# A last graph pass that softmaxes its edges while it gathers them, in a two-layer graph network kernel

## The chip, the cores and the metric

One core of a Trainium2 chip runs the whole program. The metric is device time in microseconds (us) of one execution: 3219.77, the median of 3 runs (3218.48 to 3219.83). TensorE is PE, VectorE DVE, ScalarE ACT, GpSimd POOL, SyncE SP; a q behind the name is the engine's sequencer or queue.

## What is computed

3125 nodes with 256 features, 50,000 edges sorted by destination, 8 edge types. Both layers normalize x, then add a graph part and a linear-attention part; then each adds an MLP (a mixture of experts, and one for the nodes picked by top-k). The graph part of layer 0 is an attention over edges with 8 heads and typed weights; that of layer 1 is a convolution and then an attention with one head:

```python
xw = x @ W
e = leaky_relu((xw @ a_src)[src] + (xw @ a_dst)[dst], 0.2)
m = segment_max(e, dst)
ex = exp(e - m[dst]); s = segment_sum(ex, dst)
agg = segment_sum((ex / (s[dst] + 1e-16))[:, None] * xw[src], dst)
```

with a self loop added to each node. The change is about this last attention ("the last pass"), and the attention of layer 0 ("the first pass").

## The kernel before, in words

Edges lie in NB = 196 blocks of BLK = 256, each on K2 = 2 times 128 partitions. Nodes lie in NT = 25 tiles of 128. A *pair* is a block and a tile that has edges in it; there are G = NB + NT - 1 = 220. A pass goes through the pairs in order. For each block POOL issues two indirect gathers of 128 rows of the source nodes (392 in a pass); for each pair DVE multiplies the rows by the edges' weights (`weigh`), PE multiplies by a one-hot matrix of the destinations that ACT makes (`hots`, five pairs at a time, an Abs and a Relu), and DVE adds the product to the tile's sums (`add_up`, two pairs behind). Engines run in order, each through its own list, and wait on semaphores. The passes are three stages of their own, with a barrier of all engines between stages:

- `attend` (440 to 1003 us), the first pass: the softmax is done online, inside the pass. Pairs go in 14 chunks of CH = 16. Each gathered row carries the source's scores. ACT copies them out as the rows land (`fetch`, FREE = 22 pairs ahead), and the softmax of a chunk is spread over its LEAD = 6 pairs before it (`softmax`, steps i = 0 to 6): PE turns and sums the scores, DVE runs two scans under masks of where one destination ends (`mask`, which PE spreads to 16 x 8 rows with `c.slide` and `e.pair`, into PSUM), carries between blocks, exponent on ACT, back to edges (`w_kept`); step 6 makes the factor by which the old sums fade. A ring of RING = 28 blocks holds the rows. A small product (`mix`) rides along, one tile in 8 pairs.
- `convolve_and_mix` (1815 to 2312 us), which needs no softmax.
- the last pass (2362 to 2971 us): `score2` first finds each edge's source and target scores by one-hot matmuls, from index rows read back from DRAM; `segment_softmax` does the softmax of all edges at once; `aggregate` then goes through the pairs with a ring of SLOTS2 = 20 blocks, and an MLP rides along (`MlpRide`: 103 steps spread over 208 pairs, PE products with Gelu on ACT between). SP frees a block of the ring thus:

```python
if LAG <= b < NB - slots + LAG:
    pairs = sp.value_load(e.upto[0:1, b - LAG:b - LAG + 1], min_val=1, max_val=G)
    sp.wait_ge(weighted, pairs)
    sp.sem_inc(freed, 1)
```

Ahead of the last pass `gcn_to_gat` (2312 to 2362 us) makes `xw` and the two scores of each node. `find_groups` (53 to 131 us) finds blocks, pairs and masks; `project0` (165 to 440 us) makes the rows of the first pass; `route_and_share` (1003 to 1239 us) sends tokens to experts.

## Time and profile before

| | |
|---|---|
| median of 3 runs | 3219.77 us |
| the profiled execution | 3219.89 us |
| its span, first to last instruction | 3218.0 us |
| mean granted clock of PE | 0.868 |
| first pass, first gather to last matmul | 440.0 to 1001.7 us |
| last pass, first gather to last matmul | 2362.5 to 2969.5 us |

The profile is of one execution. Its 1.9 us beside the span lie before the first and behind the last instruction. Times below count from the span's start. PE, PEld (its weight load), DVE, ACT and POOL are busy only while an instruction runs; waiting and DMA issuing of SP and ACT don't count.

### The profile page before, as it was taken

To read this page: it belongs to the slowest core of one execution; us is meant where nothing else is said; L and a number is where in the kernel's file an instruction comes from. 1 tells how busy PE (TensorE), PEld (TensorE's weight loads), DVE (VectorE), ACT (ScalarE), POOL (GpSimd) and SP (SyncE) were. 2 spreads that over 40 slices of the span, in tenths; PEclk is the share of its full clock that TensorE was granted. 3 is DMA by queue.
4 is the path that set the end of the run, shared out by engine and by line. 5 is a ranking of instruction groups with operands and counts; after the bars stand their busy time and mean duration, and the time that the engine had idled before them with its cause. 6 is when DMAs were issued, how large, how long until landed. Compare 5 with 4: busy or idle time off the path is not lost. (4 is left out here: it accounts for less than half of the span.)

```text
span 3218.0 us, 44601 instructions
## 1 busy us (share of the span) xinstructions
PE 2481.7 (77%) x12282; PEld 1848.6 (57%) x12282; DVE 1432.4 (45%) x3430; ACT 1058.0 (33%) x2707; POOL 1378.1 (43%) x1389
## 2 busy tenths in 40 slices
PE   2399945777776998999995788787566788776896
PEld 2366524544544776888884455454455666554575
DVE  4664415656656220000004311233467665555767
ACT  1012224444443112232222444444410654443220
POOL 1012247777760041000004577777640677776210
PEclk7599977878877899999998799889765999998898
DMA  5035544444430013656563433333276233333101
GB/s 187 6 123 167 177 126 112 114 113 111 115 98 29 1 65 127 193 183 194 182 195 108 123 105 106 106 106 105 72 250 220 83 100 102 103 102 97 61 1 40
DMA packets 241045, 370.76 MB, mean 115 GB/s; under 512 B 65140, under 2 KB 171073, under 8 KB 240836
## 3 DMA queue, kind: packets, MB, share of 16 engines
q0 software_dynamic: 63632, 179.42, 18.9%
q1 hardware_dynamic: 147694, 157.81, 15.5%
q10 hardware_dynamic: 29510, 31.06, 2.8%
q8 instruction: 93, 1.52, 0.2%
q14 instruction: 116, 0.95, 0.1%
HBM read 306.56 MB, written 61.61 MB: 114 GB/s over the span
## 5 line engine op out<-in xcount | busy, mean ns | idle before, releaser
L1089 POOL DMA_INDIRECT ag_rows<-rows,e_bsrc x392 | 392.5, 1001 | 245.6 <-SPq L1100 109.6
L1310 POOL DMA_INDIRECT at_rows<-values,e_brow x392 | 395.1, 1008 | 144.2 <-issue 96.3
L2539 POOL DMA_INDIRECT cm_rows<-rows,e_bsrc x392 | 371.9, 949 | 145.6 <-issue 85.7
L1386 PE MATMUL at_part<-at_msg,x 128*128 128x265 f32 x880 | 279.4, 464 | 82.4 <-DVE at_msg L1541 51.1
L2619 PE MATMUL cm_part<-cm_rows,cm_one 128*128 x880 | 263.5, 436 | 100.0 <-SPq L2546 77.8
L1115 PE MATMUL banks<-ag_msg,ag_one 128*128 128x258 f32 x880 | 242.1, 410 | 103.9 <-DVE ag_msg L1148 53.9
L2619 PEld LDWEIGHTS cm_part<-cm_rows,cm_one 128*128 128x128 f32 x880 | 170.0, 210 | 185.2 <-issue 166.0
L1386 PEld LDWEIGHTS at_part<-at_msg,x 128*128 128x128 f32 x880 | 183.5, 225 | 156.2 <-DVE at_msg L1541 75.9
L2058 POOL DMA_INDIRECT je_y<-expert_out,slots x50 | 48.5, 969 | 521.6 <-POOLq L75 506.7
L1115 PEld LDWEIGHTS banks<-ag_msg,ag_one 128*128 128x128 f32 x880 | 167.1, 200 | 164.8 <-issue 74.2
L2742 DVE TENSOR_TENSOR h<-h,cm_part 128x256 f32 x220 | 92.4, 420 | 360.8 <-PE cm_part L2619 331.8
L1984 PE MATMUL x_up<-x_xt,x_w 128*128 128x256 f32 x1024 | 228.1, 381 | 7.5 <-DMA x_b<-in_L_ffn_b2p 7.5
L1995 PE MATMUL x_down<-x_w,x_hid 128*128 128x256 f32 x1024 | 229.6, 382 | 4.5 <-ACT x_hid L2014 0.6
L2035 DVE TENSOR_TENSOR x_y<-x_down,x_b 128x256 f32<-128x256 f32 x64 | 27.2, 425 | 456.7 <-PE x_down L1995 456.7
L2014 ACT ACTIVATE x_hid<-x_up,x_b 128x256 f32<-128x256 f32 x256 | 121.4, 474 | 331.9 <-PE x_up L1984 331.9
L1984 PEld LDWEIGHTS x_up<-x_xt,x_w 128*128 128x128 f32 x1024 | 195.7, 191 | 34.7 <-issue 7.8
L1995 PEld LDWEIGHTS x_down<-x_w,x_hid 128*128 128x128 f32 x1024 | 191.9, 190 | 37.1 <-ACT x_hid L2014 12.3
L2630 ACT ACTIVATE cm_one<-iota,e_local 128x128 f32<-128x128 f32 x440 | 133.2, 387 | 182.5 <-PE cm_part L2619 172.5
L830 PE MATMUL p_ring<-cat,xnt 128*128 128x512 f32 x400 | 183.5, 601 | 0.4 <-DVE p_vals L887 0.4
L1541 DVE TENSOR_TENSOR at_msg<-at_rows,at_w 128x528 f32<-128x528 f32 x220 | 155.0, 705 | 38.5 <-PE at_part L1386 18.6
L1125 ACT ACTIVATE ag_one<-iota,e_local 128x128 f32<-128x128 f32 x440 | 133.3, 387 | 116.0 <-PE banks L1115 116.0
L1396 ACT ACTIVATE x<-iota,e_local 128x128 f32<-128x128 f32 x440 | 133.3, 388 | 104.6 <-PE at_part L1386 97.1
(619 smaller groups left out, 4200.3 us busy)
## 6 DMA issues: line engine op xcount, KB each, us to landing
x_w<-in_L_ffn_W1p SPq DMA_DIRECT2D x32, 1024.0 KB
x_w<-in_L_ffn_W2p SPq DMA_DIRECT2D x32, 1024.0 KB
values<-p_hv ACTq DMA_DIRECT2D x25, 1088.0 KB, 5.0
p_brow<-local_row SPq DMA_DIRECT2D x44, 320.0 KB, 3.6
xn_acc<-local_row SPq DMA_DIRECT2D x44, 320.0 KB
xn_acc<-low_row SPq DMA_DIRECT2D x49, 256.0 KB
expert_in<-z_z POOLq DMA_DIRECT2D x8, 1024.0 KB
x_xr<-expert_in SPq DMA_DIRECT2D x32, 256.0 KB, 2.7
```

The source lines that it names most:

```text
L830: last = pe.matmul(ring[:, b, :], xnt[:, k, t * P:(t + 1) * P], cat[:, k, b * 512:(b + 1) * 512], start=(k == 0), stop=(k == DC - 1))
L1089: pool.indirect_dma_start(rows[:, b % slots, k, :], None, table, bass.IndirectOffsetOnAxis(index[:, k, b:b + 1], 0)).then_inc(gathered[b % ...
L1115: last = pe.matmul(part[:, n % deep, 0:wide], one[:, j % 2, k, u, :], msg[:, n % 4, k, :], start=(k == 0), stop=(k == K2 - 1))
L1125: last = act.activation(one[:, j % 2, k, u, :], c.iota[:], ACT.Abs, bias=e.local[:, k, j * U + u:j * U + u + 1], scale=-1.0)
L1310: pool.indirect_dma_start(rows[:, b % RING, k, :], None, table, bass.IndirectOffsetOnAxis(e.block_row[:, k, b:b + 1], 0)).then_inc(gathere ...
L1386: last = pe.matmul(part[:, n % deep, 0:wide], one[:, n // U % 2, k, n % U, :], msg[:, n % 4, k, :], start=(k == 0), stop=(k == K2 - 1))
L1396: last = act.activation(one[:, j % 2, k, u, :], c.iota[:], ACT.Abs, bias=e.local[:, k, j * U + u:j * U + u + 1], scale=-1.0)
L1541: dve.tensor_tensor(msg[:, n % 4, :, 0:VW].rearrange("p k (h w) -> p k h w", w=HW), row.rearrange("p k (h w) -> p k h w", w=HW), w[:, pc % ...
L1984: last = pe.matmul(up_ps[:, f % 3, 0:GM], w1[:, b, k, f * P:(f + 1) * P], xt[:, b, k, :], start=(k == 0), stop=(k == DC - 1))
L1995: last = pe.matmul(down_ps[:, j, 0:D], hid[:, f, j * P:(j + 1) * P], w2[:, b, f, :], start=(f == 0), stop=(f == fb - 1))
L2539: pool.indirect_dma_start(rows[:, b % SLOTS, k, :], None, table, bass.IndirectOffsetOnAxis(e.block_src[:, k, b:b + 1], 0)).then_inc(gather ...
L2619: last = pe.matmul(part[:, n % deep, :], one[:, n // U % 3, k, u, :], rows[:, bass.ds(at[u] % SLOTS, 1), k, :].squeeze(1), start=(k == 0), ...
```

## The change

The last pass becomes `attend_last`, built like `attend`: `score2`, `segment_softmax` and `aggregate` go. Rows of `rows2` get a 257th column, the source's score. `gcn_to_gat` scatters each node's two values (target score, and self-loop score) to the place of its first edge in `spread_rows` (`start`, made by ten small DVE operations and two matmuls in `route_and_share`). `attend_last` loads these, scans them along the edges (`whole`), writes them as `block_rows`, gathers them by pair, writes `pair_rows`, and each chunk loads its part. The ring has 28 blocks; the pass keeps three accumulators, two one-hot units and additions two pairs behind. In `attend` the masks come from DRAM (`pairs`, stored in `project0`) to SBUF instead of through PE to PSUM; there are five accumulators and messages, additions come four pairs behind, and three one-hot units. `find_groups` loses the masks and rows that only the old last pass used. In the ride of the MLP one accumulator stands for two. The zeroing of `expert_in` also clears `spread_rows`.

```diff
@@ -639,25 +600,6 @@
                                             step[:, h, 1:BLK + 1][:, ::-1], 0.0, ALU.min, ALU.min))
             dve.tensor_scalar(one_run[:], e.pair[:, :, 2 * BLK], 0.0, None, ALU.is_equal).then_inc(runs_made, 1)
 
-            link(dve.tensor_scalar(edge[:], edge[:], NEG, None, ALU.mult))
...
-            link(dve.tensor_scalar(e.over_this[:], this[:], -1.0, -NEG, ALU.add, ALU.mult))
             dve.wait_ge(runs_kept, 1)
...
@@ -768,11 +710,15 @@
         def _(sp):
             sp.dma_start(wq[:], a["L0_mix_W_qkv"].rearrange("(k p) j -> p k j", p=P)[:, :, 0:P]).then_inc(loaded, 16)
             sp.dma_start(wo[:], a["L0_mix_W_out"]).then_inc(loaded, 16)
+            for q in range(H0):
+                for h in range(2):
+                    sp.dma_start(pairs[h * HALF:(h + 1) * HALF, q, :], e.pair[:, h, :]).then_inc(pair_stored, 16)
             units = local_row.rearrange("(b g) e -> b (g e)", g=U)
...
             else:
                 pe.wait_ge(self.shaped, (lo // 2 + 1) * self.fb)
-                if t >= 2:
-                    pe.wait_ge(self.added, t - 1)
-                else:
-                    pe.wait_ge(*self.gate)
+                if t:
+                    pe.wait_ge(self.added, t)
                 for f in range(self.fb):
-                    last = pe.matmul(self.down_ps[:, t % 2, 0:D], self.hid[:, f, (t - lo) * P:(t - lo + 1) * P], w2[:, f, :],
...
                 if i == 0:
...
                         for k in range(K2):
                             last = pe.matmul(turn[0:q, k * P:(k + 1) * P], of[:, k].rearrange("p n h -> p (n h)"), c.ident[:],
                                              start=(n == 0 and k == 0), stop=(n == 1 and k == K2 - 1))
                     last.then_inc(scored, 1)
-                    halves = [h for h in range(2) if lo < (h + 1) * HALF and lo + m > h * HALF]
-                    for z, cut in enumerate((slice(0, BLK + 1), slice(BLK + 1, 3 * BLK + 1))):
-                        for h in halves:
-                            at = CH + lo - h * HALF
-                            last = pe.matmul(mask[0:q, z, 0:cut.stop - cut.start],
-                                             c.slide[0:HALF, at:at + m, :].rearrange("p n h -> p (n h)"),
-                                             e.pair[:, h, cut], start=(h == halves[0]), stop=(h == halves[-1]))
-                    last.then_inc(spread_out, 1)
                 if i == 1:
...
+                        last = act.activation(ones[j % 3][:, k, u, :], c.iota[:], ACT.Abs, bias=e.local[:, k, j * U + u:j * U + u + 1], scale=-1.0)
                 last.then_inc(apart, 1)
                 act.wait_ge(apart, j + 1)
-                act.activation(one[:, j % 2], one[:, j % 2], ACT.Relu, bias=c.ones[:, 0:1], scale=-1.0).then_inc(hot, 1)
+                act.activation(ones[j % 3], ones[j % 3], ACT.Relu, bias=c.ones[:, 0:1], scale=-1.0).then_inc(hot, 1)
+
+            def take_mask(pc):
+                lo, m = CHUNKS[pc]
+                act.dma_start(mask[0:m * H0, pc % 2, :], pairs[lo:lo + m].rearrange("n h w -> (n h) w")).then_inc(mask_in[pc % 2], 16)
...
+            take_mask(0)
+            take_mask(1)
...
+            hots(1)
...
+                if n >= behind_by:
+                    if (n - behind_by) % U == 0:
+                        tiles = several(nc, mybir.EngineType.DVE, e.tile, n - behind_by, U, NT)
+                    add_up(n - behind_by, tiles[(n - behind_by) % U])
+
+
+FETCHED = 8
+LAST_RING = 28
...
+def attend_last(nc, c, e, spread_rows, token_rows, block_rows, pair_rows, pairs, table, acc, ride, loads):
...
+    deep = 3
+    wide = D + 2
...
+        @block.gpsimd
+        def _(pool):
+            for h in range(2):
+                pool.indirect_dma_start(heads[:, h, :], None, token_rows, bass.IndirectOffsetOnAxis(e.head[:, h:h + 1], 0)).then_inc(heads_in, 16)
+            for b in range(NB):
+                if b == FETCHED:
+                    pool.wait_ge(block_stored, 32)
+                    for h in range(2):
+                        pool.indirect_dma_start(pair_sc[:, h, :], None, block_rows,
+                                                bass.IndirectOffsetOnAxis(e.row[0:HALF, h:h + 1], 0)).then_inc(pair_in, 16)
+                if b >= LAST_RING:
+                    pool.wait_ge(freed, b - LAST_RING + 1)
+                for k in range(K2):
+                    pool.indirect_dma_start(rows[:, b % LAST_RING, k, :], None, table,
+                                            bass.IndirectOffsetOnAxis(e.block_src[:, k, b:b + 1], 0)).then_inc(gathered[b % LAST_RING], 16)
...
+        @block.sync
+        def _(sp):
+            for h in range(2):
+                sp.dma_start(starts[:, h].rearrange("p e z -> p (e z)"),
+                             spread_rows[h * BH * BLK:(h + 1) * BH * BLK].rearrange("(b e) z -> b (e z)", e=BLK)).then_inc(spread_in, 16)
+            for to, of in loads:
+                sp.dma_start(to, of, allow_slow_non_contiguous=True).then_inc(ride_loaded, 16)
+            sp.wait_ge(filled, 4)
+            for h in range(2):
+                sp.dma_start(block_rows[h * BH:(h + 1) * BH], whole[:, h].rearrange("p z e -> p (z e)")).then_inc(block_stored, 16)
+            sp.wait_ge(pair_in, 32)
+            for h in range(2):
...
+                if i == 0:
+                    if pc:
+                        pe.wait_ge(w_kept, pc)
+                    pe.wait_ge(copied, lo + m)
+                    for k in range(K2):
+                        last = pe.transpose(turn[0:m, k * P:(k + 1) * P], src[:, pc % 2, k, 0:m], c.ident[:])
+                    last.then_inc(scored, 1)
...
+                ride.multiply(pe, n)
...
+        @block.scalar
+        def _(act):
+            def hots(j):
+                if j >= 2:
+                    act.wait_ge(multiplied, (j - 1) * U)
...
+            def take_chunk(pc):
+                lo, m = CHUNKS[pc]
+                act.dma_start(sc[0:m, pc % 2, :], pair_rows[lo:lo + m]).then_inc(chunk_in[pc % 2], 16)
+                act.dma_start(mask[0:m, pc % 2, :], pairs[lo:lo + m, 0, :]).then_inc(chunk_in[pc % 2], 16)
...
+            def fetch(n):
...
+                act.wait_ge(ready, b + 1)
+                act.copy(src[:, pc % 2, :, j:j + 1], rows[:, bass.ds(b % LAST_RING, 1), :, D:D + 1].squeeze(1)).then_inc(copied, 1)
+
+            def softmax(pc, lo, m, i):
+                if i == 3:
+                    act.wait_ge(shifted, pc + 1)
+                    act.activation(s[0:m], s[0:m], ACT.Exp, scale=-1.0).then_inc(exped, 1)
...
+                    act.activation(fade[:], small[:, 0:1], ACT.Exp).then_inc(fade_kept, 1)
...
+            for n in range(-LEAD, G):
+                if n >= 0 and n % U == 0 and n + U < G:
+                    hots(n // U + 1)
+                if n + FREE < G:
+                    fetch(n + FREE)
+                if n in step_of:
+                    softmax(*step_of[n])
+                if n >= 0:
+                    ride.shape(act, n)
...
+                    dve.tensor_tensor(fwd[0:m, :], sc[0:m, now, 0:BLK], turn[0:m, 0:BLK], ALU.add).then_inc(summed_up, 1)
+                    dve.wait_ge(summed_up, pc + 1)
+                    dve.scalar_tensor_tensor(out=s[0:m, 0, :], in0=fwd[0:m, :], scalar=SLOPE, in1=fwd[0:m, :],
+                                             op0=ALU.mult, op1=ALU.max).then_inc(leaked, 1)
+                    dve.wait_ge(leaked, pc + 1)
+                    dve.tensor_tensor_scan(fwd[0:m, :], apart_by[:, 0:BLK], s[0:m, 0, :], 0.0, ALU.add, ALU.max).then_inc(scanned, 1)
+                    dve.wait_ge(scanned, 2 * pc + 1)
+                    dve.tensor_tensor_scan(top[0:m, ::-1], apart_by[:, 1:BLK + 1][:, ::-1], fwd[0:m, ::-1], 0.0,
+                                           ALU.add, ALU.max).then_inc(scanned, 1)
...
+                    dve.wait_ge(w_kept, pc + 1)
+                row = rows[:, bass.ds(b % LAST_RING, 1), :, 0:D].squeeze(1)
+                of = w[:, pc % 2, :, j, :]
+                dve.tensor_copy(msg[:, n % 4, :, D:wide], of)
+                dve.tensor_tensor(msg[:, n % 4, :, 0:D], row, of[:, :, 0:1].broadcast_to([P, K2, D]), ALU.mult).then_inc(weighted, 1)
...
+            dve.memset(acc, 0.0).then_inc(cleared, 1)
+            dve.wait_ge(spread_in, 32)
+            dve.wait_ge(heads_in, 32)
+            dve.tensor_copy(starts[:, :, 0, :], heads[:]).then_inc(headed, 1)
+            dve.wait_ge(headed, 1)
+            for h in range(2):
+                for z in range(2):
+                    dve.tensor_tensor_scan(whole[:, h, z, :], e.keep[:, h, :], starts[:, h, :, z], 0.0, ALU.mult, ALU.add).then_inc(filled, 1)
+            dve.wait_ge(cleared, 1)
+            dve.wait_ge(pair_stored, 32)
+            dve.wait_ge(ride_loaded, 16 * len(loads))
...
+                        pe.matmul(place_ps[:, D + NT * NX:D + NT * NX + NT], c.ones[:], degree[:], start=True, stop=True).then_inc(summed, 1)
 
         @block.scalar
...
@@ -1881,6 +1900,16 @@
                 link(dve.tensor_tensor(row[:, n], row[:, n], c.valid[:], ALU.mult))
                 link(dve.tensor_tensor(row[:, n], row[:, n], spare[:, n], ALU.add))
             dve.tensor_copy(slots[:], row[:]).then_inc(placed, 1)
+            link(dve.tensor_copy(deg[:], place_ps[:, D + NT * NX:D + NT * NX + NT]))
+            link(dve.tensor_tensor_scan(before_it[:], c.ones[:, 0:NT], deg[:], 0.0, ALU.mult, ALU.add))
+            link(dve.tensor_tensor(before_it[:], before_it[:], deg[:], ALU.subtract))
...
+            link(dve.tensor_copy(start[:], before_it[:]))
...
                 dve.tensor_copy(out[:, t, :], prod[:, t % 3, 0:D + 2]).then_inc(kept, 1)
-
-            dve.memset(target[:, NT], 0.0)
...
+                    of = slice(t - U + 1, t + 1)
+                    dve.wait_ge(kept, t + 1)
+                    dve.tensor_copy(tgt[:, of, 0], out[:, of, D + 1])
...
+                    dve.wait_ge(chain, g + 1)
+                    dve.scalar_tensor_tensor(out=tgt[:, of, 1], in0=both[:, of], scalar=SLOPE, in1=both[:, of],
+                                             op0=ALU.mult, op1=ALU.max).then_inc(leaked, 1)
+
             for t in range(NT):
...
+        @block.gpsimd
+        def _(pool):
+            for t in range(NT):
+                if t % U == 0:
+                    pool.wait_ge(leaked, t // U + 1)
+                pool.indirect_dma_start(spread_rows, bass.IndirectOffsetOnAxis(start[:, t:t + 1], 0), tgt[:, t, :], None).then_inc(spread, 16)
+            pool.wait_ge(spread, 16 * NT)
...
                 sp.wait_ge(kept, lo + U)
-                sp.dma_start(table[lo * P:(lo + U) * P].rearrange("(t p) d -> p t d", p=P), out[:, lo:lo + U, 0:D]).then_inc(stored, 16)
+                sp.dma_start(table[lo * P:(lo + U) * P].rearrange("(t p) d -> p t d", p=P), out[:, lo:lo + U, 0:D + 1]).then_inc(stored, 16)
+                sp.wait_ge(leaked, lo // U + 1)
...
-                with together(nc):
-                    *made, ride_ready = score2(nc, c, e, target, own, local_row, low_row, s2, source, banks, shared, loads)
-                    gate, down_ps = segment_softmax(nc, "sm2_", c, e, 1, 2, s2, source, scores, banks, *made)
-                    aggregate(nc, "ag2_", c, e, e.block_src, rows2, 1, scores, acc, SLOTS2, banks, gate,
-                              MlpRide(xnt, x, ACT.Gelu, weights, down_ps, gate), ride_ready)
+                attend_last(nc, c, e, spread_rows, token_rows, block_rows, pair_rows, pairs, rows2, acc, MlpRide(xnt, x, ACT.Gelu, weights), loads)
```

## Rows read from the trace of the kernel before

**Rows 1.** The page: busy time of each engine over the whole span.
```profile
PE 2481.7 (77%) x12282; PEld 1848.6 (57%) x12282; DVE 1432.4 (45%) x3430; ACT 1058.0 (33%) x2707; POOL 1378.1 (43%) x1389
```
**Rows 2.** Windows: length; busy PE, PEld, DVE, ACT, POOL; PE clock, DMA share, GB/s.
```profile
967.00:1003.00 36.00, 26.70 (x94) 17.34 (x92) 24.95 (x61) 12.49 (x32) 0.00 (x0) 0.81 0.00 1
2362.00:2505.00 143.00, 78.00 (x1660) 69.25 (x1660) 107.48 (x315) 12.44 (x29) 41.86 (x40) 0.52 0.74 241
2505.00:2972.00 467.00, 367.23 (x1492) 286.86 (x1492) 271.02 (x710) 220.81 (x544) 350.69 (x352) 0.95 0.34 100
```
**Rows 3.** Single lines: min/median/max ns, first to last start, for gathers and their matmuls.
```profile
L1310 POOL DMA_INDIRECT at_rows<-values,e_brow x392: 945/949/1489, 440.0 to 952.9; - x196
L1386 PE MATMUL at_part<-at_msg,x x880: 384/388/810, 492.9 to 1001.7; 128*128 128x265 f32 x176
L2539 POOL DMA_INDIRECT cm_rows<-rows,e_bsrc x392: 945/949/966, 1815.2 to 2305.3; - x196
L1089 POOL DMA_INDIRECT ag_rows<-rows,e_bsrc x392: 945/949/1482, 2362.5 to 2963.3; - x196
L1115 PE MATMUL banks<-ag_msg,ag_one x880: 378/381/798, 2506.5 to 2969.5; 128*128 128x258 f32 x176
```
**Rows 4.** Waits in the last pass: total us, times, longest.
```profile
POOL ag_rows L1089 <- SPq L1100: 109.6, 64, 90.4
```
**Rows 5.** Waits in the first pass, the same columns.
```profile
POOL at_rows L1310 <- SPq L1321: 22.9, 75, 0.3
DVE at_s L1476 <- ACT at_slope L1426: 89.0, 13, 14.4
```
**Rows 6.** Timeline of the first pass's end: start, length, engine, line, idle before.
```profile
967.18 0.60 PE L1334 MATMUL at_turn<-ident,at_src 128*96 128x128 f32 x4
...
996.87 5.26 PE L1386 MATMUL at_part<-at_msg,x 128*128 128x265 f32 x20 [0.53 <-issue]
```
**Rows 7.** Groups by line: the work that rides along in either pass.
```profile
L1213 PE MATMUL banks<-xnt,ff_w 128*128 128x256 f32 (+1 forms) x312 | 84.4, 396 | 0.0
L1223 PE MATMUL banks<-ff_w,mr_hid 128*128 128x256 f32 x300 | 69.6, 382 | 1.2 <-ACT mr_hid L1235 1.2
L1378 PE MATMUL at_mix<-g,xnt 128*128 128x256 f32 x100 | 32.5, 455 | 0.0
```
**Rows 8.** Window of line 1115 alone: PE and PEld busy, clock, DMA.
```profile
2560.00:2580.00 20.00, 12.02 (x50) 9.31 (x50) 1.00 0.33 98
```
**Rows 9.** Timeline of ScalarE at the first Gelu of the last pass.
```profile
2517.29 1.28 ACT L1235 ACT_TABLE_LOAD   x1
2518.59 0.47 ACT L1235 ACTIVATE mr_hid<-banks,ff_b 128x256 f32<-128x256 f32 x1
```
**Rows 10.** Timeline of `gcn_to_gat`, tile 4 and the stage's last instruction.
```profile
2335.56 0.43 DVE L2427 COPY gg_out<-gg_prod 128x258 f32<-128x258 f32 x1 [0.27 <-PE gg_prod L2455]
...
2360.30 0.20 DVE L702 CAST target<-gg_rest 128x50 bf16<-128x50 f32 x1
```
**Rows 11.** A line of 50 scatters on POOL, columns as in group 3.
```profile
L1912 POOL DMA_INDIRECT expert_in<-xn,slots x50: 959/963/1080, 1155.4 to 1217.7; - x50
```
**Rows 12.** Timeline of `find_groups` around the removed stretch.
```profile
112.24 0.42 DVE L642 TENSOR_SCALAR g_edge<-g_edge 98x512 f32<-98x512 f32 x1
...
114.19 0.33 ACT L545 COPY g_runrows<-g_turn 1x220 f32<-1x220 f32 x1
...
119.31 0.24 DVE L662 MEMSET e_same<- 1x220 f32 x1
```
**Rows 13.** Timeline of `route_and_share` behind the slot chain.
```profile
1156.95 8.86 PE L1724 MATMUL ff_down<-ff_w,ff_hid 128*128 128x256 f32 x32 [1.97 <-DVE x L1791]
```
**Rows 14.** DMA issues: engine, count, KB each, median us to landing.
```profile
p_brow<-local_row SPq DMA_DIRECT2D x44, 320.0 KB, 3.6
ff_w<-in_L_mix_w_fc SPq DMA_DIRECT2D x2, 768.0 KB, 6.2
```
**Rows 15.** The first matmuls of `project0`, columns as in group 3.
```profile
L795 PE MATMUL p_ring<-cat,xnt x100: 379/379/766, 165.0 to 188.2; 128*128 128x256 f32 x100
```

800 lines of the change are left out of this document (308 added, 492 removed).

## The prediction

> **What bounds the kernel now.** The page shows no engine that is busy all the way: PE leads with 77% of the span, POOL has 43% [rows 1]. An average over such different stages decides nothing here, so I read the two changed passes by themselves, first each pass's gathers and matmuls, then the waits, then the timeline at the ends.
>
> In the first pass POOL issues 392 gathers from 440.0 to 952.9, one each 1.312 us, the last matmul starts at 1001.7 [rows 3]. Its waits for a free block are 75 times 0.3 us [rows 5], which is the plain step from one instruction to the next: POOL is never held up, and the pass is as long as its gathers (512.9) and a tail of 48.8 behind them. The tail is what the online softmax costs: pairs follow 22 behind the gathers. At chunk starts DVE waits 89.0 us in 13 times for scores that have yet to land [rows 5], so the pairs have some time to spare.
>
> In the last pass POOL starts at 2362.5, fills the ring of 20 blocks and then stands still for 90.4 us [rows 4], while DVE does `score2` and the softmax: in 2362 to 2505 POOL is busy 41.9 of 143 us [rows 2]. From 2506.5 on gathers set the pace again, until 2963.3, and the last matmul starts 6.2 us later [rows 3]. So this pass has one gather train broken by a hole, and hardly a tail: 607.0 us from the first gather to the last matmul. A gather alone costs 1.253 us in the convolution (490.1 us / 391), where DVE does little, and 1.312 in the first pass [rows 3].
>
> **The change part by part.** The sum is made against the profiled execution, 3219.9 us (0.1 over the median).
>
> *The gather train.* The hole goes; POOL issues 2 + 392 + 2 indirect DMAs. 395 intervals by 1.312 are 518.2 us; by 1.253 they would be 495. I take the first pass's step, since DVE's work is nearly the same. At block 8 POOL waits for `block_stored`. It gets there after 18 steps, 23.6 us. Ahead of it lie a clear of the sums, two loads, a copy, four short scans and two stores, which on SP's queue stand behind 1.5 MB of weights (768 KB land in 6.2 us [rows 14]): by these some 15 to 20 us. Cost nothing, up to 10 if the cover fails; the chunk data follow 30 us before they are used. The new scans under masks in SBUF read two SBUF inputs. A pass with DVE's full work has gathers 0.06 us slower than the convolution, 23 us in 392 [rows 3]; the scans are about a sixth of such work, so I price them at 4 us in the first pass, where masks came from PSUM, and count them as part of the step of 1.312 in the last. The Trainium skill, page "SBUF — State Buffer", section "Who interferes with whom", says that such a DVE instruction contends with a GpSimd one that reads SBUF. The step of 1.253 against 1.312 in rows 3 agrees. By the rule applied to every new two-input instruction, the last pass would take up to 8 us more, an estimate.
>
> *What a chunk costs.* From the turn of the last chunk's scores at 967.18 to 1001.7 the first pass runs 18 pairs and one chunk softmax with no gather in its way [rows 6, 3]: 34.5 us. Five pairs without softmax take 5.26 [rows 6], so 16 pairs with softmax are 34.5 - 2 x 1.05 = 32.4. PE is busy 26.7 of these 36 us [rows 2]; the rest is engines waiting for each other's softmax steps. The last pass puts the MLP into it: (84.4 + 69.6) / 220 = 0.70 us of PE for each pair in place of 0.15 for the mix (32.5 / 220) [rows 7], 8.8 us in a chunk. And ACT now goes between Exp and Gelu: Exp at steps 3 and 6, a Gelu in between and after, so four table loads in a chunk, 1.28 us each [rows 9], 5.1 us. Nothing hidden, a chunk costs 46.3; all hidden in the 9 us where PE idles, 32.4. PE with the MLP but no softmax runs 12.5 pairs in 20 us at full clock (50 records, four to a pair [rows 8]), 25.6 us for 16, which leaves room for about 3 of PE's own softmax work and its waits. `down` with one accumulator waits at most for DVE's add in one pair of sixteen, some 0.8 us. I take 37.5: it is nearer to the low end because PE's MLP products stand in its queue just where it waited for DVE.
>
> *The length of the last pass.* By gathers: 518.2, then 14.3 (952.9 to 967.18) and 34.5 x 37.5 / 32.4 = 39.9 behind the last: 572.4. By pairs: the first matmul comes 52.9 after the first gather [rows 3] and here 4 steps later, 58.1; then 220 / 16 = 13.75 chunks of 37.5, 515.6: 573.7. Two limits as close as these add to each other now and then; I put 5 on top: 579. Before it was 607.0: -28.0.
>
> *The start of the last pass.* Five tiles are kept at 2335.56 + 0.43 [rows 10]; three small operations later the first scatter goes, at 2336.6. Before, 50 scatters took 62.3 / 49 = 1.27 us each [rows 11]; tiles come each 1.09 us at most, so POOL sets the pace: 25 x 1.27 = 31.8, to 2368.4. With 2.8 to land and the 2.2 us between the stage's last instruction and the first gather (2360.30 to 2362.5 [rows 10, 3]) the gathers start at 2373.4: +11. Landing of 8-byte rows is not shown; 0 to 5 more.
>
> *`find_groups`.* The removed stretch on DVE runs from 112.24 to 119.31. DVE then waits for ACT's copy, which ends at 114.52 [rows 12], so 4.8 of the 7.1 us are gained. What is removed ahead of the gather of `packed` lay under that gather: nothing.
>
> *`route_and_share`.* Two small matmul groups and ten linked DVE operations come ahead of DVE's next addition, for which PE already waits 1.97 us [rows 13]: 10 x 0.22 by the tiny operations of such a chain and 0.8 for PE: +3, bounds 0 and 3.
>
> *The first pass.* POOL issues without a break, so three one-hot units and deeper accumulators can shorten only the tail. The 18 pairs could fall from 34.5 toward 18 x 1.25; the chains of the one softmax stay. I take -5 there and +4 for the masks in SBUF: -1, bounds -12 and +5. The masks' 14 loads sit on ACT's queue two chunks ahead.
>
> *`project0`, start.* SP stores 16 x 169 KB of masks ahead of the first index rows. At 3.6 us for 320 KB [rows 14] that is at most 30 us, against 23 of other work (165.0 to 188.2 [rows 15]): 0, up to +7. The clear of `spread_rows` lies under the first stage's weights. The slide matrix goes from a stage that waits for `x`: nothing.
>
> Sum: 11 - 28.0 - 4.8 + 3 - 1 = -19.8, so 3200.1.
>
> **Rivals.**
>
> *The pairs become the bound (slower).* Place: PE's and ACT's queues in `attend_last`. Beyond 37.5 us each further us per chunk costs 13.75. Everything else brings 8.2 us more than the pass's own length, so the kernel breaks even when the pass takes 598.8: at 39.3 us a chunk; by 39.8 it is slower by 0.2%. At 42, some 10 of the 13.9 us exposed, the pass takes 635.6 and the kernel 3257; with nothing hidden 694.7, 3316. For it: 26.7 of 36 us of PE [rows 2] before 8.8 are added, and ACT stopping at `hots` until PE has finished five pairs. Against it: the spare time at chunk starts [rows 5], and that MLP and pairs ran together at 1.6 us a pair [rows 8]. Here the Trainium skill speaks against the change: "ScalarE: Activation LUTs", section "What ACT_TABLE_LOAD costs", gives about 2.66 us for each switch (load and drain) and advises batching by set. By it a chunk's four switches are an estimated 10.6 us, a chunk 51.8 with nothing hidden, and the kernel about 3391. The row disagrees: the load ends at 2518.57 and the Gelu starts at 2518.59 [rows 9], so the rule gets no chance beyond this rival's.
>
> *Nearly all hides (faster than forecast).* A chunk of 34: the pass is 518.2 + 14.3 + 34.5 x 34 / 32.4 = 568.7, the first pass gains 8: 3219.9 - 38.3 + 11 - 4.8 + 3 - 8 = 3183. For it: PE waits for DVE in the softmax, and the last pass's softmax has 16 rows where the first has 128, so its turns and carries are shorter.
>
> *POOL stands at block 8.* A stall of 10 us for `block_stored` moves the whole train: 3210. For it: the stores behind 1.5 MB. Against it: 23.6 us of cover.
>
> *The hole only moves.* If gathers of the new pass were themselves late or slower (rows of 1028 bytes), the step would show it; the first pass's rows of 1088 bytes cost 0.01 us more than the last pass's of 1024 in rows 3. I give this no chance of its own.
>
> **How the numbers follow.** A pass of 565 to 592 us, the forecast: 0.48, its own range 3186 to 3213. Nearly all hides: 0.20. Block 8: 0.05. A chunk between 39 and 39.8, no change: 0.08. Pairs bound: 0.19. 0.2% is 6.4 us, about what a measurement of this kernel can tell from none. Faster, below 3213.4: 0.70, with a part of the 0.05 given away to offsets elsewhere; within 0.2%: 0.10; slower: 0.20. The predicted time is 3200. The range takes in the fast case with its bounds elsewhere, 3172, and the slow rival up to a chunk of 40.3 us, 3232; left out are the far part of the slow rival, about 0.14, and 0.04 below.
>
> **What the profile will show.** POOL's gathers of the last pass start at 2371 (2373.4 - 4.8 + 3 - 1) and run with steps of 0.3 and no wait over 1 us, block 8 included; the last one issued some 520 us after the first; the last matmul some 55 after that. DVE's longest waits at chunk starts are for scores, not for weights. About 50 table loads. The first pass keeps its 513 us of gathers, with a tail near 44. If POOL waits for SP in the last pass for tens of us, pairs are the bound and I am too low. A chunk's length without gathers, from the last chunk's turn to the end, tells it: 39.9 us for 18 pairs is the forecast.

## The result, and the profile after

The changed kernel takes 3242.8 us (median of 4 runs, 3239.2 to 3244.5) beside 3219.8 before: a ratio of 1.0069, interval 1.0052 to 1.0087. Slower by 0.7%, where I forecast 0.6% faster and gave slower a chance of 0.20. Its profiled execution took 3239.2 us, with a span of 3237.4: 19.4 more than before. All runs below but `spaced` fell on chips where the kernel before itself takes 3700 to 3730 us, so they are compared with the profile after only in stretches that run alike on both; `half` says which those are.

The page, and single lines of the two gather passes (first the gathers, then the matmuls of each pass; columns as in [rows 3]):

```profile
PE 2450.6 (76%) x10786; PEld 1818.6 (56%) x10786; DVE 1394.2 (43%) x3442; ACT 1161.4 (36%) x3011; POOL 1421.6 (44%) x1419
```

```profile
L1012 POOL DMA_INDIRECT at_rows<-values,e_brow x392: 945/949/1479, 433.3 to 947.9; - x196
...
L1079 PE MATMUL at_part<-at_msg,x x600: 384/388/810, 486.0 to 991.5; 128*128 128x265 f32 x150
...
L2447 POOL DMA_INDIRECT cm_rows<-rows,e_bsrc x392: 943/949/1222, 1809.6 to 2300.1; - x196
...
L1357 POOL DMA_INDIRECT al_rows<-rows,e_bsrc x392: 943/949/2778, 2372.8 to 2922.9; - x196
...
L1430 PE MATMUL al_part<-al_msg,al_one x880: 378/381/801, 2426.9 to 2989.6; 128*128 128x258 f32 x176
```

Against [rows 3] these starts and ends give where the 19.4 us are:

| stretch | before | after | change | forecast |
|---|---|---|---|---|
| start to the first pass's first gather (`find_groups`, `project0`) | 440.0 | 433.3 | -6.7 | -4.8 |
| first pass, first gather to last matmul | 561.7 | 558.2 | -3.5 | -1 |
| its end to the convolution's first gather (`route_and_share`) | 813.5 | 818.1 | +4.6 | +3 |
| the convolution's gathers | 490.1 | 490.5 | +0.4 | 0 |
| its last gather to the first of the last pass's train | 57.2 | 70.1 | +12.9 | +11 |
| last pass, first of the train to last matmul | 607.0 | 619.4 | +12.4 | -28 |
| the rest | 248.5 | 247.8 | -0.7 | 0 |

The last pass's train now begins with the two gathers of scores at 2370.2; from the first gather of rows, 2372.8, which the expectations below count from, the pass takes 616.8. Only one row is far off: the last pass. Its hole of 90.4 us [rows 4] is gone, as the change says, but its gathers run over 550.1 us, not some 518, and the last matmul comes 66.7 us behind the last of them. The waits show who holds them (total us, times, longest):

```profile
POOL al_rows L1357 <- issue: 104.6, 343, 0.3
...
ACT mr_hid L935 <- PE al_up L915: 71.8, 27, 7.6
...
POOL al_rows L1357 <- SPq L1379: 39.5, 49, 4.4
PE al_part L1430 <- DVE al_msg L1570: 37.9, 21, 3.2
...
PE al_down L923 <- ACT mr_hid L935: 29.3, 9, 5.3
DVE xn_acc L1578 <- ACT al_fade L1476: 26.9, 8, 5.0
DVE al_msg L1569 <- ACT al_w L1468: 20.6, 9, 3.3
```

POOL waits 49 times for SP, up to 4.4 us, that is for a free block, and so for the pairs: the sign that the prediction had named for "pairs are the bound and I am too low". From the first matmul to the last there are 562.7 us in 220 / 16 = 13.75 chunks: 40.9 us each, where I took 37.5 and had put the break-even at 39.3. That is the rival "the pairs become the bound", and with its own sum: 58.1 + 13.75 x 40.9 = 620.5, beside 619.4 measured (the first matmul came 56.7 us into the train).

The stretch of the pairs (columns as in [rows 2]), the groups of the MLP's products as in [rows 7], and its table loads:

```profile
2427.00:2990.00 563.00, 428.25 (x1674) 326.34 (x1674) 336.54 (x1019) 325.75 (x843) 365.20 (x352) 0.85 0.31 85
```

```profile
L915 PE MATMUL al_up<-xnt,ff_w 128*128 128x256 f32 (+1 forms) x312 | 96.6, 439 | 0.0
L923 PE MATMUL al_down<-ff_w,mr_hid 128*128 128x256 f32 x300 | 83.9, 438 | 29.3 <-ACT mr_hid L935 29.3
...
L935 ACT ACT_TABLE_LOAD x27 | 34.6, 1283 | 3.7 <-issue 3.3
L1463 ACT ACT_TABLE_LOAD x14 | 18.0, 1283 | 0.2
L1476 ACT ACT_TABLE_LOAD x13 | 16.7, 1283 | 0.2
```

PE is busy 428.3 of 563 us, 76%, no more than in the old pass (79% in [rows 2]), at a granted clock of 0.85 beside 0.95. The products of the MLP are the same, yet they take 439 and 438 ns each where they took 396 and 382, so the MLP holds PE (96.6 + 83.9) / 220 = 0.82 us a pair and not the 0.70 that I took from [rows 7]. There are 54 table loads, 3.9 in a chunk.

How loads and waits meet in one chunk: the timeline of all engines around a chunk's two Exps, cut to the rows that matter (columns as in [rows 6]).

```profile
2717.23 1.28 ACT L1463 ACT_TABLE_LOAD   x1
...
2718.53 0.63 ACT L1463 ACTIVATE al_s<-al_s 16x512 f32<-16x512 f32 x1
...
2719.74 3.03 ACT L1440 ACTIVATE al_one<-iota,e_local 128x128 f32<-128x128 f32 x10 [0.58 <-PE al_part L1430]
...
2722.80 1.36 ACT L1443 ACTIVATE al_one<-al_one,ones 128x1280 f32<-128x1280 f32 x1
...
2724.15 0.21 ACT L1468 COPY al_w<-al_turn 128x64 f32<-128x64 f32 x1
...
2724.46 0.32 DVE L1569 COPY al_msg<-al_w 128x4 f32<-128x4 f32 x1 [2.83 <-ACT al_w L1468]
...
2725.38 1.59 PE L1430 MATMUL al_part<-al_msg,al_one 128*128 128x258 f32 x4 [2.02 <-DVE al_msg L1570]
...
2726.34 1.28 ACT L1476 ACT_TABLE_LOAD   x1
...
2727.63 0.17 ACT L1476 ACTIVATE al_fade<-al_small 128x1 f32<-128x1 f32 x1
```

The large Exp starts only behind its load. The copy of the new weights stands behind five pairs' one-hots; DVE waits 2.83 us for it and PE 2.02 for DVE. The small Exp, on which DVE's first addition of the chunk waits, again comes behind a load.

### The profile page after: what moved, and what is told of

Same layout as the page of the kernel before. It is cut to its first block and busy times, and to the rows that moved or that the text cites. A ratio compares the mean times of both kernels' runs of the same rounds, so it can differ in the third digit from the quotient of the medians.

```text
span 3237.4 us, 41564 instructions
## 1 busy us (share of the span) xinstructions
PE 2450.6 (76%) x10786; PEld 1818.6 (56%) x10786; DVE 1394.2 (43%) x3442; ACT 1161.4 (36%) x3011; POOL 1421.6 (44%) x1419
## 3 DMA queue, kind: packets, MB, share of 16 engines
q0 software_dynamic: 64768, 180.50, 19.4%
## 5 line engine op out<-in xcount | busy, mean ns | idle before, releaser
L1357 POOL DMA_INDIRECT al_rows<-rows,e_bsrc x392 | 404.5, 1032 | 144.1 <-issue 104.6
L1430 PE MATMUL al_part<-al_msg,al_one 128*128 128x258 f32 x880 | 256.6, 432 | 50.3 <-DVE al_msg L1570 37.9
L1430 PEld LDWEIGHTS al_part<-al_msg,al_one 128*128 128x128 f32 x880 | 182.6, 215 | 91.1 <-DVE al_msg L1570 45.6
L1079 PE MATMUL at_part<-at_msg,x 128*128 128x265 f32 x600 | 185.2, 456 | 50.4 <-DVE at_msg L1243 29.9
L1079 PEld LDWEIGHTS at_part<-at_msg,x 128*128 128x128 f32 x600 | 124.4, 222 | 92.8 <-DVE at_msg L1243 39.0
L1440 ACT ACTIVATE al_one<-iota,e_local 128x128 f32<-128x128 f32 x440 | 133.2, 388 | 103.3 <-PE al_part L1430 84.3
L706 POOL TENSOR_TENSOR p_of<-p_rid,e_rel 128x640 f32<-128x640 f32 x44 | 55.5, 1262 | 251.5 <-DVE p_pick L820 193.6
```

The costliest lines, as they stand in the source:

```text
L1079: last = pe.matmul(part[:, n % deep, 0:wide], ones[n // U % 3][:, k, n % U, :], msg[:, n % ahead, k, :], start=(k == 0), stop=(k == K2 - 1))
L1357: pool.indirect_dma_start(rows[:, b % LAST_RING, k, :], None, table, bass.IndirectOffsetOnAxis(e.block_src[:, k, b:b + 1], 0)).then_inc(ga ...
L1430: last = pe.matmul(part[:, n % deep, 0:wide], one[:, n // U % 2, k, n % U, :], msg[:, n % 4, k, :], start=(k == 0), stop=(k == K2 - 1))
L1440: last = act.activation(one[:, j % 2, k, u, :], c.iota[:], ACT.Abs, bias=e.local[:, k, j * U + u:j * U + u + 1], scale=-1.0)
```

## The experiments

**`spaced`: half of the table loads gone, the MLP packed closer.**

```diff
+        free = [n for n in range(6, G - 6) if n % CH not in (13, 14, 15, 0)]
         for i, step in enumerate(steps):
-            self.due[6 + i * (G - 12) // len(steps)].append(step)
+            self.due[free[i * len(free) // len(steps)]].append(step)
```

> Edit: the changed kernel with the MLP's steps of the last pass moved: none falls on the four pairs of a chunk from the step with the large Exp to the step with the small one, so that the two Exps need one table load and the way back to Gelu another; nothing is left out. Theory T (table loads lie on a chunk's path): two of four loads of 1.28 us go, and the copy of the weights and the small Exp have no Gelu between them; a chunk falls from 40.9 by 2.5 to 4 us, the last pass from 616.8 to 570 to 585. Rival (waits between PE and ScalarE for one-hots and copies): the pass changes by under 8 us; steps packed into 12 pairs of 16 may even cost more.

This one ran where the kernel before took 3223.8 us. It took 3241.6 us.

```profile
L1431 PE MATMUL al_part<-al_msg,al_one x880: 378/382/801, 2430.8 to 2991.0; 128*128 128x258 f32 x176
```

```profile
2431.00:2991.00 560.00, 437.78 (x1673) 332.69 (x1674) 337.01 (x1019) 291.77 (x817) 369.98 (x351) 0.84 0.32 85
...
L1431 PE MATMUL al_part<-al_msg,al_one 128*128 128x258 f32 x879 | 277.3, 457 | 57.1 <-DVE al_msg L1571 42.1 <-issue 8.9 <-ACT al_one L1444 5.8
```

560.2 us of pairs, 40.7 a chunk, and 614.7 from the first gather of rows, beside 616.8, with 28 loads in the pass for 54. Theory T had asked for 2.5 to 4 us less. The window over the pairs (columns as in [rows 2]) and the group of their products (as in [rows 7]) show both a gain and a loss. PE's idle time fell from 9.8 to 8.9 us a chunk ((560.2 - 437.8) / 13.75, beside (562.7 - 428.3) / 13.75 after). Its busy time rose from 31.1 to 31.8: the pairs' own products took 457 ns each and not 432, at a granted clock of 0.84. What fewer loads gave, the packing took back.

**`noride`, `relu`, `three`, `three_b`, `noride_b`, `three_c`, `ring25`: the full pass with one thing changed.** The MLP's steps left out; Relu for Gelu; a third one-hot unit (three times); a ring of 25 blocks.

```diff
-                ride.multiply(pe, n)
...
-                if n >= 0:
-                    ride.shape(act, n)
...
-                    ride.add(dve, n)
```

```diff
-                if j >= 2:
-                    act.wait_ge(multiplied, (j - 1) * U)
+                if j >= 3:
+                    act.wait_ge(multiplied, (j - 2) * U)
...
-                if n >= 0 and n % U == 0 and n + U < G:
-                    hots(n // U + 1)
+                if n >= 0 and n % U == 0 and n + 2 * U < G:
+                    hots(n // U + 2)
```

> Edit: the changed kernel with the MLP's steps left out of the last pass (no products, no Gelu, no additions to x; its weights are still loaded). The output lacks that MLP. The last pass of the changed kernel took 616.8 us from the first gather to the last matmul, and its pairs 562.5 from first to last matmul: 40.9 a chunk of 16. Theory A (the MLP is what makes pairs the bound): a chunk needs 32 to 34 and gathers set the pace, so the last gather comes 518 to 525 after the first with no wait of POOL over 1 us, and the pass takes 565 to 580. Rival (the softmax chain with three accumulators and two one-hot units is too slow by itself): a chunk stays at 37.5 or more, POOL still waits for SP, the pass is over 590.

> Edit: the changed kernel with Relu in place of Gelu in the last pass's MLP, so that ScalarE has no table to load between it and Exp; the output has another activation there. Theory T (table loads are on the path of a chunk): four loads of 1.28 us go, 5.1 us, so a chunk falls from 40.9 to 36 and the pass from 616.8 to 575 to 585. Rival (ScalarE has slack for them, PE and the waits between engines are the bound): a chunk falls by under 1.5 us, the pass stays above 596.

> Edit: the changed kernel with a third one-hot unit in the last pass, made two units ahead of its use, as in the new first pass; everything else as it was. Theory L (ScalarE is locked to PE: it may make the next five one-hots only when PE has finished the last five, so what stands behind them in its queue, the copies that the next chunk's turn needs, comes late, 3.7 us at 2707.5): PE's wait for the copies goes, some 2 to 4 us of a chunk, and the pass falls from 616.8 to 580 to 595. Rival (table loads or the softmax's own chain): the pass changes by under 8 us.

> Edit: the same kernel as in the run named three, on another chip, since on the first one every kernel, the one before included, took some 500 us longer, with waits of 5 to 19 us all over the gathers' passes. The changed kernel with a third one-hot unit in the last pass, made two units ahead of its use. Theory L (ScalarE is locked to PE by its two units, so the copies behind them in its queue come late): the last pass falls from 616.8 to 580 to 595, the kernel's ratio to before from 1.0069 to 0.996 to 1.000. Rival (table loads, or the softmax's own chain): the pass changes by under 8 us, the ratio stays over 1.004.

> Edit: as the run named noride, since that one ran while every kernel took some 500 us longer: the MLP's steps left out of the last pass (output without that MLP). Both theories want the gathers to set the pace, 518 to 525 us with no wait of POOL over 1 us, and a pass of 565 to 580; if it stays above 590, the softmax chain alone is too slow.

> Edit: as the runs named three and three_b, which ran while every kernel took some 500 us longer: a third one-hot unit in the last pass, made two units ahead. Theory L (ScalarE locked to PE, PE waits 29 us in 12 times for the copies before a turn and 12 for one-hots): a chunk falls from 40.9 to 38 to 39.5 and the pass from 616.8 to 580 to 600. Rival: under 8 us.

> Edit: the changed kernel with a ring of 25 blocks in the last pass instead of 28; the copies run 22 pairs ahead, so 3 blocks are to spare instead of 6. Theory C (the two paces are coupled by the ring): the pass gets longer by 10 to 40 us. Theory P (pairs alone set the pace): POOL waits for blocks more often, but pairs stay within 4 us of 562.7.

On these chips every pass of gathers is stretched, the first pass and the convolution as well, which the edits don't touch (656 to 694 and 567 to 575 us of gathers, beside 515 and 490). From first gather to last matmul the last pass took 696.6 and 701.5 us without the MLP, 745.9 with Relu, 756.3, 749.6 and 755.4 with the third unit, 741.9 with the short ring. With the same kernel 7 us apart, and with no run of the changed kernel itself there, only the MLP's 50 us stand out. `three_b` was timed: 0.9984 of before, interval 0.9953 to 1.0015. The short ring (one run) is not slower than those with the long one, which speaks against a coupling through the ring, though weakly, since it was compared with runs that have a third unit. For the rest these runs are inconclusive, and the numbers expected of them, made for the other chips, can't be held against them.

**`half`: the pairs' own pace.** Half of the last pass's gathers are left out, and SP's wait for a block is set to match, so that pairs never wait for a row.

```diff
-                for k in range(K2):
+                for k in range(K2 if b < LAST_RING else 1):
                     pool.indirect_dma_start(rows[:, b % LAST_RING, k, :], None, table,
...
-                sp.wait_ge(gathered[b % LAST_RING], 16 * K2 * (b // LAST_RING + 1))
+                sp.wait_ge(gathered[b % LAST_RING], 16 * (K2 + b // LAST_RING))
```

> Edit: the changed kernel with half of the last pass's gathers left out: both rows of a block are gathered for the first 28 blocks, then only the first half of each block (the other half keeps old rows, so the sums are others). Pairs then never wait for a row, and the pass shows their own pace. Theory P (the pairs themselves are the bound, 40.9 us a chunk with nothing from the gathers): pairs stay at 555 to 563 us from first to last matmul. Theory C (pairs and gathers each need 37 to 38 a chunk and hold each other up through a ring with 6 blocks to spare): the pairs fall to 525 or less, 38 a chunk.

Two views of it: the pass's matmuls, and the window over them.

```profile
L1430 PE MATMUL al_part<-al_msg,al_one x880: 377/382/801, 2802.6 to 3355.1; 128*128 128x258 f32 x176
```

```profile
2803.00:3355.00 552.00, 425.87 (x1673) 325.17 (x1673) 335.61 (x1019) 324.65 (x841) 165.89 (x168) 0.85 0.16 42
```

552.5 us, 40.2 a chunk; busy times and clock are those of the profile after (428.3 us of PE, 0.85). The first five of the twelve intervals between the turns of successive chunks are 46.2, 40.4, 41.6, 37.4, 41.2 here and 46.9, 40.7, 41.7, 39.2, 42.6 in the profile after; the other seven differ by at most 2.2. So with few gathers the stretch runs here as it does on the other chip, and it is in such stretches that the next runs are read. Theory P is borne out, not C: the pairs alone need 40.2, 2.5 us in all under P's range, and gathers add 0.7. The 5 us that I had put on for two close limits were no longer the question, since the limits were not close.

**`half_noride`, `half_relu`, `half_three`, `half_all`, `half_defer`: what makes the 40.2.** Each is `half` with one more edit, and one execution: no MLP; Relu for Gelu; the third unit; the third unit with PE's and DVE's order changed; Gelus held back. The order of `half_all`, where the call ahead of the softmax's step takes the first layer's products alone:

```diff
-    deep = 3
+    deep, ahead, behind_by = 3, 5, 3
...
             for n in range(-LEAD, G):
+                if n > 0:
+                    ride.multiply(pe, n, False)
                 if n in step_of:
                     softmax(*step_of[n])
...
-                if n in step_of:
+                if n < 0 and n in step_of:
                     softmax(*step_of[n])
                 if 0 <= n < G:
...
                     weigh(n, blks[n % U])
+                    if n in step_of:
+                        softmax(*step_of[n])
...
-                if n >= 2:
+                if n >= behind_by:
```

and of `half_defer`:

```diff
+HELD = (13, 14, 15, 0)
...
+            while step[3] is not None and at % CH in HELD:
+                at += 1
...
-                if n >= 0:
+                if n >= 0 and (n % CH not in HELD or n > CHUNKS[-1][0]):
                     ride.shape(act, n)
+                if n > 0 and n % CH == 0:
+                    for held in range(n - 3, n + 1):
+                        ride.shape(act, held)
```

> Edit: as the run named half (half of the last pass's gathers left out, so that pairs show their own pace, 40.2 us a chunk there), and the MLP's steps left out of the last pass too. Theory M (the MLP's 8.8 us of PE work a chunk is not hidden at all): a chunk falls to 31.5 to 33, pairs 433 to 454 us in all. My forecast's rule (about half of it hides where PE waits anyway): 35 to 36.

> Edit: as half, with Relu in place of Gelu in the MLP, so no table is loaded in the pass. Theory M: under 1 us a chunk, 39.2 to 40.2. Rival T (table loads cost 5.1 a chunk in full): 35 to 36.

> Edit: as half, with a third one-hot unit, made two units ahead. Theory L (PE waits for copies and one-hots that stand behind ScalarE's wait for PE): 1.5 to 3 us less, a chunk of 37 to 38.7. Rival: within 0.7 us of 40.2. If the third unit does nothing here, it was the DVE's and PE's own order.

> Edit: as half_three, and three changes of order: the MLP's first-layer products stand ahead of the softmax's step in PE's queue, DVE weighs a pair before it takes that pair's softmax step, and its additions come three pairs behind instead of two (five messages, a ring of 27). Theory O (PE stands idle behind DVE's softmax steps because its own work is queued behind the wait, and DVE's next message is queued behind its softmax step): a chunk falls to 33 to 36. Rival (the chain of the softmax from engine to engine sets the pace whatever stands where): over 38.

> Edit: as half (half of the last pass's gathers left out), and ScalarE holds back the at most two Gelus that fall on the four pairs of a chunk from the large Exp to the small one, until after the small one; PE's products stay evenly spread, only a second-layer product may move by up to four pairs. Nothing else is left out. Theory T (the loads ahead of the two Exps are on the path, and spaced gave its gain back by packing): a chunk falls from 40.2 to 38 to 39, pairs to 523 to 537 us. Rival (two loads instead of four bring nothing, since only a pass with none lets ScalarE keep up): 39.7 to 40.5.

The window over the pairs, without the MLP, then with Relu:

```profile
2799.00:3249.00 450.00, 313.94 (x1059) 204.31 (x1058) 312.36 (x968) 223.89 (x709) 172.36 (x168) 0.78 0.19 51
```

```profile
2786.00:3293.00 507.00, 409.09 (x1673) 312.61 (x1674) 335.24 (x1019) 255.59 (x789) 167.36 (x168) 0.88 0.17 46
```

The groups of PE in the same two windows: the pairs' own products without the MLP, then with Relu, then the MLP's two layers with Relu.

```profile
L1429 PE MATMUL al_part<-al_msg,al_one 128*128 128x258 f32 x877 | 294.0, 483 | 85.9 <-DVE al_msg L1567 63.1 <-issue 13.5 <-ACT al_one L1442 8.2
```

```profile
L1430 PE MATMUL al_part<-al_msg,al_one 128*128 128x258 f32 x879 | 251.4, 425 | 50.2 <-DVE al_msg L1570 36.2 <-issue 7.7 <-ACT al_one L1443 6.2
L915 PE MATMUL al_up<-xnt,ff_w 128*128 128x256 f32 (+1 forms) x312 | 94.5, 432 | 0.0
L923 PE MATMUL al_down<-ff_w,mr_hid 128*128 128x256 f32 x300 | 73.0, 395 | 8.8 <-ACT mr_hid L935 5.2 <-issue 3.5 <-DVE x L945 0.2
```

| run | first to last matmul | a chunk | PE busy | PE idle | loads |
|---|---|---|---|---|---|
| `half_noride` | 2798.5 to 3249.4 | 32.8 | 22.8 | 10.0 | 1 |
| `half_relu` | 2786.0 to 3293.1 | 36.9 | 29.8 | 7.1 | 1 |
| `half_defer` | 2803.0 to 3336.3 | 38.8 | 29.9 | 8.9 | 28 |
| `half` | 2802.6 to 3355.1 | 40.2 | 31.0 | 9.2 | 54 |
| `half_three` | 2790.3 to 3347.0 | 40.5 | 31.2 | 9.3 | 54 |
| `half_all` | 2803.2 to 3354.8 | 40.1 | 30.7 | 9.4 | 54 |

(Columns three to five in us, by 13.75 chunks; the loads are those of the pass, and the one load of the first two runs comes ahead of the first matmul.) The MLP with Relu costs 36.9 - 32.8 = 4.1 us a chunk, Gelu's loads 40.2 - 36.9 = 3.3. `half_noride` lies in the range of theory M, but M gave the loads under 1 us and its rival T 5.1; 3.3 is neither.

Held back, half of the loads are gone and 1.4 of the 3.3 with them, as theory T expected. The edit also moves second-layer products by up to four pairs, so not all of the 1.4 need be the loads'. `spaced` had seemed to refute T; it lost to slower products what it gained in idle time.

The third unit brings nothing, so theory L falls. Theory O was not tested cleanly. `half_all` lets additions come three pairs behind but keeps three accumulators. PE's product of a pair then needs the addition of the third pair before it, which stands in DVE's queue behind the step of the softmax, and a new wait takes the place of the one for messages, 37.0 us in `half`:

```profile
PE al_part L1434 <- DVE xn_acc L1586: 54.3, 36, 3.7
```

Whether the order would help with a fourth accumulator was not run.

**`defer`, `defer_b`: the held-back Gelus with all gathers.**

> Edit: the same on the changed kernel with all of its gathers and nothing left out. Theory T: where a chunk takes 40.9 now, it takes 38.5 to 39.7, so the last pass falls by 15 to 30 us and the kernel comes to within 0.3% of the kernel before on either side, instead of 0.7% over it. Rival: no change from 1.0069.

> Edit: the same kernel as in the run named defer. By half_defer a chunk needs 38.8 us beside 40.2, so pairs still set the pace over the gathers' 37.1 to 37.7: on a chip where the kernel before takes 3220 us, the last pass falls from 616.8 to 595 to 605 and the ratio to before from 1.0069 to 1.001 to 1.004; where it takes some 3700, a ratio of 0.995 to 1.000 as before.

0.9978 of before (0.9949 to 1.0006), then 0.9964 (0.9939 to 0.9989), where before takes 3706 and 3727 us. The second is the only interval on such chips that lies below 1; it overlaps that of `three_b`, so a gain over the changed kernel is not shown there. Whether it is faster where before takes 3220 was not measured; by 38.8 + 0.7 a chunk the pass would take 54.1 + 543.1 = 597.2, and the span 3237.4 - 19.6 = 3217.8, as much as before (an estimate).

**`first`, `first_b`: the change's first pass alone on the kernel before.**

> Edit: the kernel before with the change's first pass alone: masks stored to DRAM and loaded in chunks to SBUF, five accumulators and messages, additions four pairs behind, three one-hot units; the last pass and its preparation are those of before. In the changed kernel the first pass's tail fell from 48.8 to 43.6 and its gathers took 1.7 us more, so 3.5 us are expected here, a ratio of 0.9989; storing the masks costs nothing or up to 3 us. If the first pass brought something of the 23 us of loss, this would be slower than before; I expect it is not.

> Edit: the same kernel as in the run named first, the change's first pass alone on the kernel before. On a chip where the kernel before takes 3220 us: 3.5 us less, a ratio of 0.9985 to 0.9995; elsewhere no difference from before beyond its interval.

1.0019 (0.9997 to 1.0042) and 1.0029 (1.0000 to 1.0058). The gain expected of `first` did not show there; if anything these runs are 0.2% slower. The 3.5 us of the profile after are one execution's, on the other kind of chip, where this edit was not run by itself. Their last pass is the old one, and it takes 787.4 and 783.4 us (first gather to last matmul) beside 741.9 to 756.3 in the seven runs with the new pass's MLP: on such chips the new pass is the shorter one.

## Why the prediction was wrong

**The step that failed: what the MLP puts on a chunk, and where it hides.** The prediction put 8.8 us of MLP products and 5.1 us of loads on top of 32.4, and took 37.5, "nearer to the low end because PE's MLP products stand in its queue just where it waited for DVE". The 8.8 was mis-sized. It is the MLP's 0.70 us a pair less 0.15 for the mix, but the stretch from which 32.4 was read, 967 to 1003, has no product of the mix in it. The last ones start at 960.7 and 961.0 (timeline of PE before, columns as in [rows 6]):

```profile
960.73 0.69 PE L1379 MATMUL at_mix<-bo,ones 1*128 1x256 f32 x2
```

Nothing was to be subtracted, so the rows gave 16 x 0.70 = 11.2, and 48.7 with nothing hidden.

The runs have 12.2 us of MLP products a chunk with Relu ((94.5 + 73.0) / 13.75) and 13.1 in the profile after, and 3.93 x 1.283 = 5.0 us of loads. The products show with 4.1, the loads with 3.3, gathers with 0.7, and `half_noride` needs 32.8: 40.9. Beside 37.5 this is 0.4 for the low end, 2.3 for products and loads (7.4 for 5.1), 0.7 for the gathers. Times 13.75, (40.9 - 37.5) x 13.75 = 46.8 us; less the 1.4 by which the first matmul came sooner and the 5 that I had added, this is the 40.4 by which the pass missed 579.

**Where the MLP's time goes.** Of 12.2 us only 2.9 went into PE's idle time (10.0 to 7.1). Another 5.3 came from somewhere that the prediction did not have: PE's other products took (313.9 - 241.6) / 13.75 = 5.3 us less a chunk. The pairs' own took 425 ns each with the MLP around them and 483 without, at a granted clock of 0.88 beside 0.78. The last 4.1 made the chunk longer. So PE's 9 us of idleness in [rows 2] were not a store into which 8.8 us of products could go. That the miss was not larger is luck: the hiding place took a third of what it was given, and 5.3 came back through quicker products, for which the prediction had no term.

**Where the loads' 3.3 us go.** PE's groups in `half`, beside those of `half_relu` above, place most of it (the second layer as a group, the turn as a wait):

```profile
L923 PE MATMUL al_down<-ff_w,mr_hid 128*128 128x256 f32 x300 | 84.3, 440 | 28.0 <-ACT mr_hid L935 28.0
...
PE al_turn L1410 <- ACT al_s L1463: 16.2, 8, 4.0
```

The second-layer products wait 28.0 us for Gelu's output where with Relu they were idle 8.8 us, and they take 84.3 us where they took 73.0: (19.2 + 11.3) / 13.75 = 2.2 a chunk. The turn behind the large Exp waits 16.2 for 6.2: 0.7. The second layer stands in PE's queue ahead of the pair's product, so its wait for Gelu holds the pair. Giving these products more pairs of delay was not tried by itself. Nor was the copy of the weights put ahead of the five pairs' one-hots, which hold it for 4.4 us in the chunk shown above; DVE waits 20.6 us in the pass for that copy. What sets the 9 us of idle time that stay in every run with Gelu is open beyond this.

**The chunk that was read.** The sign that the prediction named, 39.9 us from the last turn to the end, measured 38.2 (2951.4 to 2989.6), as if the forecast held, while the twelve intervals between turns are 41.6 on average. The last stretch is light: the MLP's steps end with pair 211, and it holds 6.5 us of their products where 18 average pairs hold 14.8. In `half_noride` it takes 32.2 us, which by the prediction's rule is 30.1 a chunk, beside 33.6 from turn to turn. So reading a chunk from the last stretch of the first pass was no safe rule, and that 32.4 met 32.8 is in part luck.

**The clock.** I read 25.6 us for 16 pairs with the MLP from a window at full clock [rows 8], and the MLP's share from groups taken at 0.95. In the new pass, where PE stops at each softmax step, the granted clock was 0.85 on the mean, and the MLP's busy time rose from 0.70 to 0.82 us a pair, 1.9 a chunk. `half_relu`, with less idle time, had 0.88.

**Table loads.** I priced four in a chunk, 1.28 us each. 3.9 came, at 1.283 each, and together cost 3.3: 0.86 us for each of the 53 that `half` has over `half_relu`. The Trainium skill, page "ScalarE: Activation LUTs", section "What ACT_TABLE_LOAD costs", has about 2.66 us for a switch, load and drain. By it a chunk's 3.9 would hold ScalarE for an estimated 10.4 us. The trace has the load, 1.283 us, but no drain: the next activation starts 0.02 us behind the load (2717.23 + 1.28, 2718.53), and ahead of the 14 loads of L1463 ScalarE is idle for 0.2 us in all. The page's advice to batch by table set, in its section "Table sets: the hidden batching unit", does agree in direction: 1.4 us a chunk came back in `half_defer`.

**What was right.** `find_groups`: the memset of `past` that came at 123.3 comes at 116.9, 6.4 less for 4.8, since ACT's copy, for which DVE then waits, came sooner as well. `project0` hides the stores of the masks: its share of -6.7 is -0.3. The first pass: its tail went from 48.8 to 43.6 (991.5 - 947.9), -5.2 for -5, its gathers from 512.9 to 514.6, +1.7 for +4 (one execution each; `first` and `first_b` could not confirm a gain). Block 8: the two gathers of `block_rows` were issued with no more than the usual 0.3 us ahead. `route_and_share`: +4.6 for +3. The start of the last pass (timeline of POOL):

```profile
2361.22 0.96 POOL L2379 DMA_INDIRECT spread_rows<-gg_tgt,start  x1 [0.30 <-issue]
2362.49 0.96 POOL L2379 DMA_INDIRECT spread_rows<-gg_tgt,start  x1 [0.30 <-issue]
2370.21 1.01 POOL L1347 DMA_INDIRECT al_heads<-token_rows,e_head  x1 [6.76 <-POOLq L60]
2371.52 0.99 POOL L1347 DMA_INDIRECT al_heads<-token_rows,e_head  x1 [0.30 <-issue]
2372.82 0.97 POOL L1357 DMA_INDIRECT al_rows<-rows,e_bsrc  x1 [0.31 <-issue]
```

The first of the train is at 2370.2, where I had 2371. Scatters follow each other by 1.27 us as forecast; between the last one's end and the train lie 6.8 us, where 2.8 + 2.2 were forecast.

**The chances.** The rival was named, with a break-even that holds, and got 0.19. What should have moved the chance is that half of a cost hidden was a choice between 32.4 and 46.3, whose middle, 39.4, lies on the break-even. With the mix not subtracted the top is 48.7 and the middle 40.6, above it.

## What to carry to other kernels

Idle time of an in-order engine that comes from a chain over several engines is little room for riding work: here 12.2 us of products took 2.9 from 10.0 us of it. Count a rider in full against a window that has no rider in it, and subtract another rider only where the window shows it. Look at PE's granted clock with and without the rider, since it changes what all of PE's other products cost: here it gave 5.3 us back. Read a chunk's price from turn to turn in the middle of a pass and not from its end. When a pass may be bound by either of two trains, starve one of them (half of the gathers) and read the other's own pace. And when a run changes an order, look at its waits before calling the order useless: the edit may have made a new one.

## What was not expected of the hardware

On the chips of all runs but `spaced`, five of them, the kernel before took some 480 to 510 us more. In `three_b`, whose span is 458.3 us over that of the profile after, 365 of these lie in the three passes of gathers, from first gather to last matmul (the convolution: to its last gather). In such passes instructions of the sequencers themselves take some 0.7 us for stretches of 5 to 20 us at a time, on SP, ACT and PE at once. SP's release of a block, 17 ns otherwise, in the first pass, in the profile after and in `three_b` (ns min/median/max):

```profile
L1023 SPq EVENT_SEMAPHORE  x168: 17/17/17, 494.1 to 936.3; - x168
```

```profile
L1023 SPq EVENT_SEMAPHORE  x168: 3/17/712, 520.2 to 1089.7; - x168
```

Other stages are not all alike either. `project0` ends within 2 us of where it ends after, and from the last matmul of the last pass to the end it is 248.9 us for 247.8. But between the first pass and the convolution `three_b` takes 885.1 us for 818.1, and 48 of these 67 lie between the last of the 50 scatters of `route_and_share` and the experts' first matmul. With half of the gathers gone the last pass ran nearly undisturbed: SP's release took at most 0.32 us in `half`, but up to 0.47 in `half_relu` and 0.70 in `half_noride`, so those two may be a little long. What holds the sequencers there was not found.
